# Attention kernel, images 1 to 3, slots 0 to 3: GpSimd adds two halves of the exponentials before TensorE sums them

## The reference

```python
q = layernorm(x, ln_g, ln_b).transpose(0, 3, 1, 2).reshape(b, h * w, c) @ wq + bq
o = gelu(depthwise_conv7x7_stride2(q_img) + dw_b)       # -> 16 x 16 sampling offsets
interp = grid_sample(x, grid_of(tanh(pointwise(o))))    # 256 sampled rows
qh, kh, vh = heads(q @ mq_w + mq_b), heads(k @ mk_w + mk_b), heads(v @ mv_w + mv_b)
attn = softmax(einsum('bnqd,bnkd->bnqk', qh, kh), axis=-1)   # 8 heads, 1024 queries, 256 keys
att = einsum('bnqk,bnkd->bnqd', attn, vh)                    # head width 32
z = att @ mo_w + mo_b + x
out = gelu(layernorm(z, ln_g, ln_b) @ mlp_w + mlp_b) + z
```

## Time and profile before

| | |
|---|---|
| median of 3 runs | 492.38 us (491.51, 492.38, 494.83) |
| the profiled execution | 492.23 us, its span 490.4 us |
| PE busy | 453.6 us, 92% of the span |
| DVE busy | 288.3 us, 59% |
| ACT busy | 211.8 us, 43% |
| POOL busy | 108.5 us, 22% |
| granted TensorE clock, mean | 0.993 of full speed |

### The profile page before, as it was taken

How to read it: one execution, slowest core, us unless ns; L and a number is a source line. 1 busy time by engine, 2 the same in 40 slices (tenths; PEclk the granted TensorE clock), 3 DMA queues, 4 the chain that set the end, 5 groups by cost and what they waited for, 6 DMA issues and landing times.

```text
span 490.4 us, 9348 instructions
## 1 busy us (share of the span) xinstructions
PE 453.6 (92%) x3761; PEld 317.3 (65%) x3761; DVE 288.3 (59%) x617; ACT 211.8 (43%) x338; POOL 108.5 (22%) x149
## 2 busy tenths in 40 slices
PE   6899898898999899999899999999999898988976
PEld 5767665556576566766677666766767565665755
DVE  4629456869743477577644455576646648626343
ACT  1222203553553335855144336755363674663150
POOL 6600201321021003761012003761030031000000
PEclk9999999999999999999899999999999999999999
DMA  7499758667759901473158801473145200000112
GB/s 216 105 169 117 148 99 189 109 187 94 115 93 125 236 5 41 94 87 65 45 104 110 170 1 43 90 87 66 71 71 79 86 3 2 1 3 1 43 43 87
DMA packets 30488, 42.90 MB, mean 87 GB/s; under 512 B 6075, under 2 KB 21230, under 8 KB 30446
## 3 DMA queue, kind: packets, MB, share of 16 engines
q1 hardware_dynamic: 23742, 34.95, 38.7%
q0 software_dynamic: 3584, 4.50, 3.6%
q10 hardware_dynamic: 3120, 2.86, 2.9%
HBM read 16.16 MB, written 4.19 MB: 41 GB/s over the span
## 4 chain that ended last, share of the span: by engine, by line
PE 59%; DVE 16%; DMA 12%; ACT 5%; issue 5%; POOL 2%; SPq 1%; ACTq 0%; DVEq 0%; POOLq 0%
PE ps_d L778 7%; PE ps_d L903 6%; PE ps_d L880 5%; PE ps_d L980 5%; PE ps_s L827 5%; PE ps_v L863 4%; DMA xa<-in_x_dram 4%; PE ps_v L869 4%; PE ps_d L922 4%; PE ps_t L846 4%; PE ps_d L798 4%; PE ps_d L766 3%; DVE mx L1647 3%; DMA q_st<-mx_t 2%; DMA th_st<-mx_t 2%
## 5 line engine op out<-in xcount | busy, mean ns | idle before, releaser
L1257 ACT ACTIVATE prob<-ps_t 128x1024 f32<-128x1024 f32 x64 | 65.4, 1022 | 93.5 <-PE ps_t L846 92.0
L1647 DVE TENSOR_REDUCE mx<-ps_s 128x4 f32<-128x1024 f32 x64 | 78.1, 1221 | 22.6 <-PE ps_s L827 21.5
L1951 POOL DMA_DIRECT2D q_st<-mx_t x64 | 33.7, 528 | 246.7 <-ACT mx_t L1249 227.3
L778 PE MATMUL ps_d<-cstack,conv_w 128*32 128x256 f32 x1024 | 58.7, 380 | 1.5 <-issue 1.3
L827 PE MATMUL ps_s<-k_st,q_st 96*128 96x256 f32 x256 | 48.0, 309 | 6.2 <-DVE mx L1647 5.0
L778 PEld LDWEIGHTS ps_d<-cstack,conv_w 128*32 128x32 f32 x1024 | 34.6, 108 | 23.4 <-issue 3.8
L827 PEld LDWEIGHTS ps_s<-k_st,q_st 96*128 96x128 f32 x256 | 35.2, 189 | 18.5 <-DVE mx L1647 12.8
L846 PE MATMUL ps_t<-q_st,k_st 98*128 98x256 f32 x256 | 42.2, 287 | 3.5 <-DMA q_st<-mx_t 1.6
L846 PEld LDWEIGHTS ps_t<-q_st,k_st 98*128 98x128 f32 x256 | 35.0, 189 | 6.2 <-issue 2.8
L863 PE MATMUL ps_v<-prob,vh 128*32 128x256 f32 x512 | 34.3, 385 | 1.9 <-DVE att L1661 1.7
L1661 DVE TENSOR_TENSOR att<-ps_v,rden 128x256 f32<-128x256 f32 x32 | 13.5, 423 | 35.9 <-ACT rden L1268 35.8
(11 more groups left out here) (180 smaller groups left out, 738.8 us busy)
## 6 DMA issues: line engine op xcount, KB each, us to landing
q_st<-q_parts SPq DMA_DIRECT2D x42, 256.0 KB, 7.1
xa<-in_x_dram SPq DMA_DIRECT2D x8, 512.0 KB, 7.8
z_all<-in_x_dram SPq DMA_DIRECT2D x8, 512.0 KB, 7.9
out_dram<-z_all SPq DMA_DIRECT2D x8, 512.0 KB, 2.6
cstack<-qpad SPq DMA_DIRECT2D x22, 180.5 KB, 5.7
k_st<-cstack SPq DMA_DIRECT2D x23, 128.0 KB, 3.3
q_st<-z_all SPq DMA_DIRECT2D x6, 256.0 KB, 5.8
cstack<-att SPq DMA_DIRECT2D x6, 180.5 KB, 5.4
```

The lines of the kernel that those rows point to most:

```text
L778: ins = pe.matmul(ps[32 * k:32 * k + 32, 0, :], conv_w[:, cb * 4 + k, y, x, :], cstack[:, cb, k, y:y + HG_, x:x + WG_], start=n == 0, stop ...
L1257: drain(act.activation(prob[:, u % 2, 2 * pr:2 * pr + 2].rearrange("p h m s -> p (h m) s"), ps_t[:], ACT.Exp), t_ring, "t", b, u, pr)
L1647: drain(dve.tensor_reduce(mx[:, u % 2, half, :], ps_s[:], AX.X, ALU.max), s_ring, "s", b, u, half)
```

## The change

For the twelve units that are summed in slots 0 to 3 of images 1 to 3 (units 5, 6 and 7 of the image before and unit 0 of the image itself), a GpSimd addition writes the sum of the two key halves over the first half of `prob`, once the values have been mixed; TensorE then multiplies the ones with that one half. Two semaphores order this: `mixed_done`, raised by the last product of `values_mixed`, which GpSimd awaits, and `halves_done`, raised by the addition, which TensorE awaits ahead of the sum. The other twenty units keep both products. Line numbers behind the additions move; the fence below has the diff, cut.

```diff
+def halves_before(b, u):
+    done, s = divmod(UNITS * b + u + 3, UNITS)
+    return 4 * (done - 1) + s + 1
...
+        mixed_done = sem("mixed_done")
+        halves_done = sem("halves_done")
...
-            def values_mixed(b, u):
+            def values_mixed(b, u, added=False):
...
-                        pe.matmul(ps_v[32 * h:32 * h + 32, 0, :], vh[:, mt, hh * HD:(hh + 1) * HD],
-                                  prob[:, u % 2, h, mt, :], start=mt == 0, stop=mt == 1)
-
-            def values_summed(b, u):
-                for mt in range(2):
+                        ins = pe.matmul(ps_v[32 * h:32 * h + 32, 0, :], vh[:, mt, hh * HD:(hh + 1) * HD],
+                                        prob[:, u % 2, h, mt, :], start=mt == 0, stop=mt == 1)
+                if added:
+                    ins.then_inc(mixed_done, 1)
+
+            def values_summed(b, u, added=False):
+                if added:
+                    pe.wait_ge(halves_done, halves_before(b, u))
+                for mt in range(1 if added else 2):
                     for h in range(HQ):
                         ins = pe.matmul(ps_v[32 * h:32 * h + 32, 1, :], ones[:], prob[:, u % 2, h, mt, :],
-                                        start=mt == 0, stop=mt == 1)
+                                        start=mt == 0, stop=added or mt == 1)
...
-                    values_mixed(*unit_of(b, s, 3))
+                    values_mixed(*unit_of(b, s, 3), added=b > 0 and s < 4)
...
-                    values_summed(*unit_of(b, s, 3))
+                    values_summed(*unit_of(b, s, 3), added=b > 0 and s < 4)
...
+            def add_halves(b, u):
+                pool.wait_ge(mixed_done, halves_before(b, u))
+                part = prob[:, u % 2]
+                pool.tensor_tensor(part[:, :, 0, :], part[:, :, 0, :], part[:, :, 1, :], ALU.add).then_inc(halves_done, 1)
...
                 if unit_of(b, s, 1):
                     max_row(*unit_of(b, s, 1))
+                if b and s < 4:
+                    add_halves(*unit_of(b, s, 3))
```

## The result

| | before | after |
|---|---|---|
| median (lowest to highest) | 492.04 us (490.84 to 494.83), 6 runs | 498.1 us (496.72 to 499.49), 6 runs |
| ratio to before, 95% interval | | 1.0115 (1.008 to 1.015) |
| profiled execution, its span | 492.23 us, 490.4 | 499.49 us, 497.4 |
| granted TensorE clock, mean, same execution | 0.993 | 0.979 |

What follows compares the result with a forecast made beforehand. TensorE was taken to bound the kernel, except in slot 0, where VectorE is on the path. 4.0 us gained less 2.4 us of hold-up gives 1.6 us less: 490.8 us against the median of 492.38, range 487.8 to 494.0.

Steps and rivals of the forecast that it cites:

- The hold-up of VectorE: Slot 0, images 1 and 2: GpSimd's addition holds off VectorE's two-input SBUF instructions; cost 2.4 us.
- the third rival: Slot 0, images 1 to 3: the addition holds off zn too; 6.1 us lost against 4.0 gained, 494.5 us; chance 0.10.
- The meeting of `xln` and addition: Slot 0: xln waits for the addition's end, 1.81 us in image 1 and 0.62 us in image 2.
- The gain of TensorE: Twelve halved sums take 6.0 us off TensorE, of which 4.0 us lie on the path.
- slots 0: Images 1 to 3: turned maxima behind the sum wait for VectorE, so three shorter sums gain 0 of 1.5 us.
- slot 1 of image 3: The next mixing waits for att behind ScalarE's late exponentials, so the shorter sum gains 0 of 0.5 us.
- Half a sum: Each unit's sum is 16 records, 1.00 us on the chain; halving it saves 0.50 us.
- slot 3 of image 3: The sum leads to ScalarE's logarithm, which the earlier sum starts earlier; gain 0.5 us.
- Seven places: Slots 1 to 3 of images 1 and 2, slot 2 of image 3: TensorE on both sides; gain 3.5 us.
- The addition: GpSimd, each of twelve units: 2.36 us, hidden ahead of the sum, 0.15 us over in slot 2 of image 3.
- The second rival: GpSimd late: an addition of 3.5 us delays slot 2 of image 3 and lengthens xln's wait; 494.0 us; chance 0.08.

Runs made afterwards that it cites:

- the memset run: Kernel before plus one GpSimd memset over 128x1024 of an unused tile beside slot 0's zn in images 1 to 3; 492.7 us, one run.
- the copy: Kernel before plus one GpSimd copy over 128x512, SBUF to SBUF, beside slot 0's zn in images 1 to 3; 494.35 us, one run.
- short_only: Kernel after without additions and their waits, its twelve short sums taken over a stand-in tile of ones; 490.81 us, ratio 0.9978 to before.
- padded2: after_rd plus 8 and 16 one-column products on TensorE in slot 0 of images 1 and 2; 488.89 us, ratio 0.9904 to before.
- no_slot0: Kernel after without slot 0's three additions, whose sums take both halves on TensorE again; 491.33 us, ratio 0.9956 to before.
- filled: Kernel after plus eight spare TensorE products in slot 0 of images 1 to 3, ahead of zn's turned rows; 500.15 us, ratio 1.0179 to before.
- after_rd: Kernel after with slot 0's addition waiting for zn, xln and, in images 2 and 3, the scaling of rd; 490.94 us, ratio 0.9971 to before.
- eight: Kernel after with only eight additions: slots 1 to 3 of images 1 and 2, slots 2 and 3 of image 3; 492.96 us, ratio 1.0015.
- only_slot0: Kernel after with only slot 0's three additions, the other nine sums on TensorE as before; 499.52 us, ratio 1.0155 to before.
- after_zn: Kernel after with slot 0's addition waiting for the four zn tiles; 497.3 us, ratio 1.0091 to before.

## Why the prediction was wrong, step by step

**The hold-up of VectorE: the step that failed.** The forecast said that `zn`, with one SBUF input, "does not look as if it used a second way into SBUF", because a tile of it takes 0.35 us on the chain and one of `xln` 0.40. It gave the third rival a tenth of the chances for that. The rate was no evidence: `zn` is as slow and is held all the same, until the addition ends, and the scaling of eight elements a row likewise. The rival's price was right to the tenth (6.1 us), in part by luck: its terms were 2.1, 2.0 and 2.0 us, with the wait of `xln` in the first, where `zn` alone lost 2.56, 1.75 and 1.77, and about 5 of the 6.1 reached the time. Its time of 494.5 was not right, since it let all 4.0 us of the gain arrive and knew nothing of the clock. The meeting of `xln` and addition that the forecast did price never happened, because `zn` comes first. No row of the trace before has `zn` beside a GpSimd instruction, and the forecast bounded that case rightly at 6.1 but then chose by analogy.

The row of after shows `zn` at 2974 ns, and the memset run shows that a mere writer is enough. With these the Trainium skill agrees, page "SBUF — State Buffer", section "Who interferes with whom": it lists `tensor_scalar` among the operations that can take the pair of ports shared with GpSimd, for reading and writing, so that the later one waits out the earlier, and says that `tensor_reduce` never does (VectorE's maxima take 1.22 us in all places here too, though none begins inside an addition: they are under way when it starts). By that list `zn` was a candidate at any speed. Where it does not fit is the unheld `zn` beside the last 0.25 us of the copy, and L1727 in the earlier trace rows: either GpSimd lets go before its recorded end, or something else decides. That stays open.

**The gain of TensorE: mis-sized.** In slots 0 the forecast was right that nothing would come (TensorE idles for 0.62 us ahead of the turned maxima in image 1), and in slot 1 of image 3 too. Half a sum was taken as half of 1.00 us and is worth 0.43, since the shorter group costs 0.57. And slot 3 of image 3, priced at 0.5, gives 0.1: ScalarE's logarithm `rden` comes 8.46 us behind the mixing before and 8.35 after, where the chain has 0.90 us of "issue" on ScalarE ahead of it and no longer the sum. Seven places at 0.43 and this one make 3.1 us. short_only measures 1.6 at equal clock (known to 0.3), padded2 3.3. In between stand things that no step of the forecast had: the pause in slot 2 of image 2, 1.2 to 1.35 us; the pause of image 1, which is 0.5 us shorter in short_only than before, and 0.2 longer in no_slot0; and the transfer in slot 7 of image 1. They do not close the balance to better than some 0.7 us.

**The addition: right.** 2.36 us forecast, 2356 ns measured, hidden in all twelve places, with 0.36 us from its end to the sum in the tightest. The forecast had 0.15 to spare besides a hop back of 0.15, together 0.30. The second rival did not occur.

**The clock: in no step.** The mean clock is 0.9896 before and 0.9817 after: 0.0079 x 330 = 2.6 us by the fitted line. It is an estimate, and what lowers the clock is only argued. In image 1 the idling of 2.59 us that the hold-up causes is followed by 3.4 us at half clock, which before does not have; filled has full clock there, and its slot loses 2.5 us and not 3.1. In image 2 the trace of before has such a stretch as well. The means bear the link out in part: 0.9817 and 0.9832 where `zn` is held for the whole addition, 0.9893 in after_rd; but eight, with nothing held, has 0.9882.

**The account.** TensorE's shorter sums -1.6 (short_only), the hold-up +5.0 (only_slot0), the clock +2.6: together +6.0 us, where the medians differ by 6.1. The first two are levels at equal clock, so the clock is not counted twice. It would be with the 5.1 us by the slots of the trace, which hold image 1's stretch at half clock. That 6.0 meets 6.1 is luck to some 0.7 us: the kernel after has a level of its own, some 2.7 us above before at equal clock (known to 0.4), where the two parts make 3.4; and the six runs of before that stand beside it have a median of 492.04, the later ones 492.42 to 493.72. Besides, one stretch of 6.8 us at half clock at 90.9 us of the profiled execution lies ahead of every edit. It belongs to that execution, not to the change, and is one reason for comparing medians and not the two traces' spans.

## What to carry to other kernels

Before GpSimd gets work over SBUF, list what VectorE runs beside it, by operation and not by rate. Two inputs in SBUF (`xln`), or a tensor-scalar operation from SBUF to SBUF (`zn`, the scaling), were stopped here until GpSimd's addition was done. The reciprocal, the statistics and the additions with an input in PSUM beside it were not. Three instructions that began some 0.3 us before GpSimd's recorded end (`zn` beside the copy, twice, and L1727) were not held either. A wait that places GpSimd's work behind these costs nothing where its result is needed late, and one should then look again at what it meets next.

## What the runs showed of the hardware that I had not expected

- A tensor-scalar operation of VectorE from SBUF to SBUF was held by GpSimd at either size that met it: 2974 ns for 256 elements a row (0.40 alone), 1.91 us for 8 (0.23 alone), 1560 ns behind a memset of 0.97 us.
- The records do not tell who came first: in image 1 the held `zn` tile has a record that begins at 135.19, the addition one that begins at 135.65, when the tile should have been done. The memset of image 1 does the same: 133.90, its held tile before 133.7. So a recorded start on GpSimd is not the moment from which it holds VectorE off.
- A pause of 1.3 us stood in a convolution ahead of which TensorE's list had become 24 products shorter (six sums), and 24 one-column products, put in far ahead of it, took it out again. Another, of 0.59 to 1.63 us, stands behind record 1349 or 1350 of TensorE in every kernel here, wherever in the work that falls.
- TensorE idle for 2.6 us and then 3.4 us at 1.2 GHz in image 1, and full clock when the same stretch was filled with spare products. Yet 2.72 us of idling in after_zn had no such stretch behind it, and in image 2 of before one came behind idling of 0.57 and 0.76 us.
